# Attention: head images stacked for two batches in one set of DMAs, maxima of three heads in one reduction, TensorE's step reordered

## The reference

```python
    B, T, C = x.shape
    qkv = x @ w_attn
    q, k, v = jnp.split(qkv, 3, axis=-1)
    ...
    q = _apply_rope(q, emb)
    k = _apply_rope(k, emb)
    scale = HEAD_DIM ** (-0.5)
    wei = jnp.einsum('bhqd,bhkd->bhqk', q, k) * scale
    causal = jnp.tril(jnp.ones((T, T), dtype=bool))
    wei = jnp.where(causal[None, None], wei, -jnp.inf)
    wei = jax.nn.softmax(wei, axis=-1)
    out = jnp.einsum('bhqk,bhkd->bhqd', wei, v)
    out = out.transpose(0, 2, 1, 3).reshape(B, T, C)
    out = out @ w_proj
```

## Time and profile before

| what | us |
|---|---|
| median of 3 runs | 334.37 |
| lowest and highest run | 330.97 and 334.4 |
| the profiled execution | 332.37 |
| its span | 330.6 |
| stage A and what is ahead of it | 0 to about 123 |
| stage B | about 123 to 247 |
| feed-forward block | about 247 to the end |

### The profile page before, as it was taken

The page is one execution under the profiler, slowest core; times in us unless marked ns, Lnnn a source line. Parts: engine busy times, 40 slices in busy tenths (PEclk is TensorE's granted clock), DMA queues, the critical chain, the costliest instruction groups (busy, mean ns, idle before and its releaser), DMA issues.

```text
span 330.6 us, 6296 instructions
## 1 busy us (share of the span) xinstructions
PE 253.5 (77%) x1878; PEld 191.1 (58%) x1878; DVE 241.3 (73%) x674; ACT 138.2 (42%) x300; POOL 133.8 (40%) x133
## 2 busy tenths in 40 slices
PE   0129896976868785779998879899876969797881
PEld 0029795976757764546776667767554545454440
DVE  2999589999899988984687656767546674747453
ACT  0320022132232232355665546666765754545350
POOL 1640425758668776563232322333486430000000
PEclk9999999799999998957999979999999887896978
DMA  5900000000008950022433434341000001011011
GB/s 139 234 0 1 26 24 24 2 25 6 20 24 116 115 57 0 0 53 62 106 76 87 97 87 93 84 108 24 2 2 1 2 0 36 0 36 36 2 48 37
DMA packets 25847, 15.61 MB, mean 47 GB/s; under 512 B 3872, under 2 KB 25696, under 8 KB 25824
## 3 DMA queue, kind: packets, MB, share of 16 engines
q1 hardware_dynamic: 23568, 14.04, 21.2%
q10 hardware_dynamic: 2256, 1.29, 1.8%
HBM read 4.26 MB, written 1.57 MB: 18 GB/s over the span
## 4 chain that ended last, share of the span: by engine, by line
DVE 33%; PE 29%; SPq 18%; issue 10%; DMA 3%; ACT 2%; POOL 2%; DVEq 1%; ACTq 0%; POOLq 0%
SPq L364 13%; PE bank L1413 8%; DVE xs_ring L817 7%; PE bank L1428 7%; DVE xl_ring L868 6%; SPq L380 5%; DVE xn_ring L804 3%; DVE rest_ring L843 2%; DVE parts L1066 2%; DMA rad_bc<-in_L_conv_radius 2%; DVE gn_st L748 2%; PE bank L1306 2%; PE bank L1194 2%; PE bank L1264 1%; DMA stack<-nmax_t 1%
## 5 line engine op out<-in xcount | busy, mean ns | idle before, releaser
L921 DVE TENSOR_REDUCE nmax<-bank 128x1 f32<-128x128 f32 x192 | 55.0, 348 | 29.3 <-PE bank L1267 28.9
L490 POOL TENSOR_SCALAR_AFFINE_SELECT pt_ring<-pt_ring 128x512 f32<-128x512 f32 x48 | 30.5, 637 | 62.4 <-ACT pt_ring L618 62.4
L1168 PE MATMUL bank<-xs_ring,toep 128*128 128x192 f32 x256 | 51.3, 347 | 2.2 <-DVE xs_ring L817 2.2
L618 ACT ACTIVATE pt_ring<-bank 128x384 f32<-128x384 f32 x96 | 41.7, 487 | 20.0 <-PE bank L1283 19.3
L1168 PEld LDWEIGHTS bank<-xs_ring,toep 128*128 128x128 f32 x256 | 45.2, 203 | 3.8 <-issue 2.5
L1264 PE MATMUL bank<-stack 96*128 96x128 bf16 x192 | 35.2, 260 | 0.7 <-ACT nmax_t L607 0.4
L1267 PE MATMUL bank<-mask,ident 128*128 128x128 bf16 x192 | 35.2, 231 | 0.0
L1281 PE MATMUL bank<-stack 97*128 97x256 bf16 x96 | 23.7, 290 | 11.0 <-DMA stack<-nmax_t 7.2
L868 DVE TENSOR_SCALAR xl_ring<-tok,ln_mv,ln_rstd 128x96 f32<-128x96 f32 (+1 forms) x32 | 27.6, 920 | 2.1 <-POOL ln_rstd L467 2.1
L1031 DVE TENSOR_REDUCE amax<-parts 128x1 f32<-128x384 f32 x30 | 16.4, 552 | 16.8 <-ACT parts L672 15.7
L1413 PE MATMUL bank<-parts,w_b 96*128 96x384 f32 x60 | 28.6, 626 | 0.0
(11 more groups left out here) (145 smaller groups left out, 503.2 us busy)
## 6 DMA issues: line engine op xcount, KB each, us to landing
stack<-parts SPq DMA_DIRECT2D x96, 96.0 KB, 3.4
x_ring<-in_x SPq DMA_DIRECT2D x8, 192.0 KB, 2.5
out<-xs_ring SPq DMA_DIRECT2D x5, 288.0 KB, 2.6
stack<-in_x SPq DMA_DIRECT2D x2, 384.0 KB, 6.1
stack<-in_x ACTq DMA_DIRECT2D x2, 384.0 KB, 10.8
stack<-nmax_t SPq DMA_DIRECT2D x32, 1.5 KB
cst<-in_const SPq DMA_DIRECT2D x1, 384.0 KB, 11.3
w_in<-in_L_ffn_W ACTq DMA_DIRECT2D x2, 144.0 KB, 12.1
```

The source lines that it names most:

```text
L490: nc.gpsimd.affine_select(out=v, in_=v, compare_op=ALU.is_ge, fill=0.0, base=0, pattern=[[0, 2], [0, 2], [1, P]], channel_multiplier=-1).t ...
L618: nc.scalar.activation(pt_ring[:, s, h, :], bank[:, 3 + h % 2, 0:T + P], ACT.Exp, scale=float(HD) ** -0.5).then_inc(s_exp, 1)
L921: last = nc.vector.tensor_reduce(nmax[:, n0 % 2, HEADS * t + h:HEADS * t + h + 1], bank[:, h % 3, first:first + (t + 1) * P], op=ALU.max, ...
L1168: nc.tensor.matmul(dst, w, xs_ring[:, s, p, k].rearrange("p b c -> p (b c)"), start=(k == 0 and p == 0), stop=False)
```

## The change

It has three parts.

1. **Images of two batches.** `parts` is laid out by pairs of batches, so that the same part of two neighbouring batches lies side by side, and `stack` has three slots of two batches. `stack_images(n)` issues six DMAs of 192 KB for batches n and n+1, for even n. The runs of memory that a DMA reads are twice as long (512 bf16 values, 1 KB, where they were 512 bytes; 2 KB in the one combination whose q and k parts are neighbours). SP's order is now, for n = 4, 6, ..., 14: `max_row(n-3)`, the wait for both batches, `stack_images(n)`, `max_row(n-2)`.
2. **Maxima of three heads.** `maxima` takes heads 0 to 2 or 3 to 5 in two reductions over three banks, and `scores_q` waits once for three heads. The transposed maxima go to bank 5 instead of bank 2 (except those of batch 0), with waits that keep them apart from `transpose_o`'s output there.
3. **A step's order.** TensorE's `step_b` is `scores_k` 0, three heads of `scores_q`, `scores_k` 1, `transpose_max`, `weighted_values`, `transpose_norm`, three heads of `scores_q`, `scores_k` 2, `project_out`, `transpose_o`. DVE normalises batch n-2's output at the start of step n, where it did n-1's in the middle of it. ACT does the second pair of exponentials before it copies `o_ring`.

```diff
-        stack = sb("stack", [P, RING, HEADS, 2, T], BF16)
+        stack = sb("stack", [P, RING // 2, HEADS, 2, 2, T], BF16)
...
-        parts_v = parts[0:C, :].rearrange("c (b s k n) -> c (b s) k n", b=B, s=2, k=3)
+        parts_v = parts[0:C, :].rearrange("c (j s k u n) -> c (j s) k u n", j=PAIRS, s=2, k=3, u=2)
...
-            def stack_image(i, n0):
+            def stack_images(i, n0):
                 b, slot = n0 + RING * i, n0 % RING
                 for r, (kp, qp) in enumerate(SLOTS):
-                    q_part = parts[0:C, ds((b * 6 + qp) * T, T)]
-                    src = bass.AP(q_part.tensor, q_part.offset, [q_part.ap[0], [(3 + kp - qp) * T, 2], [1, T]])
-                    dst = stack[r * HD:(r + 1) * HD, slot, :, :, :].rearrange("d h s n -> d (h s n)")
-                    sp.dma_start(dst, src).then_inc(s_stack[slot], 16)
+                    q_part = parts[0:C, ds((b * 6 + 2 * qp) * T, 2 * T)]
+                    src = bass.AP(q_part.tensor, q_part.offset,
+                                  [q_part.ap[0], [(3 + kp - qp) * 2 * T, 2], [1, 2 * T]])
+                    dst = stack[r * HD:(r + 1) * HD, slot // 2, :, :, :, :].rearrange("d h s b n -> d (h s b n)")
+                    sp.dma_start(dst, src).then_inc(s_stack[slot // 2], 16)
...
-            for n in range(4):
-                stack_ready(0, n)
-                stack_image(0, n)
+            for n in (0, 2):
+                images_ready(0, n)
+                stack_images(0, n)
             max_row(0, 0)
-            def step_b(i, n0):
-                max_row(i, n0 - 3)
-                stack_ready(i, n0)
-                stack_image(i, n0)
-            run(sp, step_b, start=4, first=4, unroll=RING, laps=2, last=B)
+            with sp.Fori(0, 2) as i:
+                for n in (4, 6, 8):
+                    max_row(i, n - 3)
+                    images_ready(i, n)
+                    stack_images(i, n)
+                    max_row(i, n - 2)
...
-            def maxima(i, n0, h):
+            def maxima(i, n0, g):
                 b = n0 + RING * i
-                dve.wait_ge(s_sq, HEADS * b + h + 1)
-                if h == 0:
+                dve.wait_ge(s_sq, HEADS * b + 3 * (g + 1))
+                if g == 0:
                     wait(dve, s_mt, b - 1)
                 for t in range(NT):
-                    first = t * P
-                    last = nc.vector.tensor_reduce(nmax[:, n0 % 2, HEADS * t + h:HEADS * t + h + 1],
-                                                   bank[:, h % 3, first:first + (t + 1) * P],
+                    first, k = t * P, HEADS * t + 3 * g
+                    last = nc.vector.tensor_reduce(nmax[:, n0 % 2, k:k + 3], bank[:, 0:3, first:first + (t + 1) * P],
                                                    op=ALU.max, axis=AX.X, negate=True)
```

191 lines of the change are left out of this document (98 added, 93 removed).

## The result

| | before | after |
|---|---|---|
| median, 4 runs each | 334.38 us | 370.88 us |
| lowest and highest | 330.97 and 334.96 | 367.46 and 372.81 |
| the profiled execution | 332.37 | 367.46 |
| its span | 330.6 | 365.7 |

The ratio is 1.110, with a 95% interval of 1.099 to 1.122: 11% slower. The forecast was 352 us with a range to 362, so the sign was right and the size was half of it. In the profiled executions the spans differ by 35.1 us, where the forecast had 19.8.

A forecast was written before the change was run, and what follows sets the result against it. SP's issues were taken to bound the kernel, with DMA bytes next; +1.0 up to step 2, +20.2 in five rounds and -1.4 behind step 12 made +19.8 on 332.37: 352 us, range 343 to 361.

The forecast's parts named there:

- new waits: 0: Waits of `transpose_max` and `transpose_o` for bank 5 and ACT's cast: 0 us; prologue shift 0, bounds -0.5 and +1.
- maxima of three heads: 0: DVE's reductions gain 0.5 us a step, worth 0; coarser exchange with TensorE costs 0, given 5 us slack a round.
- the -1.4 behind step 12: Behind step 12 no images are in the way, so waits of 0.7 us in two steps go: -1.4 us.
- X: Stage B, time until all six image DMAs have landed: 2.7 us beside the bytes plus 9.4 of bytes, 12.1 us.
- Rival A: Transfers keep pace with their issue; a DVE loop of 5.6 us a step is near: round 11.3, 323 us, chance 0.22.
- B: Engines keep an undisturbed image's rate: bytes take 6.4 us, round 13.2, 332 us, no change; chance 0.12.
- C: SP still bounds, larger DMAs issued at half the pace (1.4 us each): round 12.3 us; no case of its own.
- The round of 17.0: Two batches in stage B: 4.1 us, X of 12.1 and 0.8 for the clock make 17.0, where 12.95 was.
- 4.1 and 0.8 for the clock: Even step's start to image issue: 2.1 us to the odd batch's row, 2.0 on SP; 0.8 for TensorE's lower clock.
- bounds of 0 and 1.7: Range for TensorE's clock loss in a round, whose 1.7 us part would take 3.4; 0.8 was taken.
- bounds of -0.5 and +1 for the prologue: Batch 1's scores behind `transpose_max` and its cast can shift by about 0.25 us either way: put at 0.

The follow-up runs named there:

- images alone: Kernel before with only the images of two batches, its old maxima and old order kept: 354.8 us, ratio 1.071.
- order alone: Kernel before with only the maxima of three heads and the new order of TensorE, DVE and ACT, images and SP's order as before: 343.3 us, ratio 1.033.

## Why the forecast had the sign right and half of the size

The difference of the spans, by the forecast's own terms:

| | forecast | images alone | order alone | the change |
|---|---|---|---|---|
| up to step 2 | +1.0 | +1.9 | +4.1 | +4.6 |
| five rounds | +20.2 | +20.2 | -0.2 | +24.7 |
| from step 12 to the last `project_out` | -1.4 | +1.1 | +5.0 | +6.5 |
| feed-forward block, unchanged | 0 | -1.4 | -0.6 | -0.6 |
| sum | +19.8 | +21.7 | +8.3 | +35.1 |

The five rounds with the images alone are 20.2 of the 35.1 us, as forecast. What failed are the terms put at nothing, *new waits: 0* and *maxima of three heads: 0*, and the -1.4 behind step 12: the stretches in which they stand are 3.6 and 7.9 us longer than forecast. In the rounds 4.5 us are missing, most of them in X.

*What bounded before*: right. Rows off SP's queue, and a step falls from 6.48 to 6.04 us. But TensorE's own step was put at 5.4 us. Its busy time in ten steps, 58.15 us, already said 5.8.

*The bytes pass at 118 GB/s in a burst, whatever their runs*: right. 1.66 us for each DMA of 192 KB, where 1.67 was forecast, and half of the bytes end the long rounds. The Trainium skill (page "DMA: Bandwidth & Descriptors", section "Bandwidth") gives 435 GB/s as the fabric's ceiling for SBUF to SBUF. No burst here comes near it, with large or small DMAs. Rival A fell, the one that this rate would have favoured, and its other leg fell too: a step of the new order takes 6.07 us where nothing holds it up, not 5.6. Rivals B and C fell as well: the last image lands 8.8 us after its issue, and SP issues the large ones at the old pace.

*The round of 17.0*: 17.9 was measured. From the step's start to the issue of the set the forecast had 4.1 and 0.8 for the clock, and the five rounds have 4.04, 5.36, 5.47, 5.48 and 4.81, 5.03 in the mean. The walk through `scores_k` 0, three heads, `scores_k` 1, the transpose, the cast and SP was right: 4.04 is the first round, at full clock. The clock then adds 1.3 to 1.4 in three rounds and 0.8 in the last, inside the forecast's bounds of 0 and 1.7. Behind the 4.57 us wait the granted clock is 0.50 for all of the next 6.4 us, not for half of them, as it was behind the wait of 1.68 us. The mis-sized term is X: 12.86 us from the first issue to the next even step in the round from 200.81, not 12.1. The first image lands after 4.1 instead of 3.7, and step n+2 begins 0.4 behind the last landing, for which the sum had no term. This is 3.8 us in five rounds.

That the images alone give rounds of 16.98, the forecast's number, is luck. There the transpose stands behind two heads and the set follows the step's start after 4.08 us, 0.8 less than the forecast's 4.9 for the new order, and the longer landing fills that up. The forecast walked the new order's path to the odd batch's row, but did not ask what that path costs against the old order's. The run with `transpose_max` put back answers: 0.9 us a round. In the trace the walk to the cast's end takes 3.6 us at half clock (195.33 to 198.89), where the old order needs 2.4 (191.29 to 193.68).

*New waits: 0*, and *maxima of three heads: 0*. These are the steps that failed. The reason given was that DVE has 5 us of slack in each round. That is true in the rounds and says nothing of the steps outside them. In step 0 the exchange of three heads (two reductions, 948 and 555 ns, in these rows)

```profile
L922 DVE TENSOR_REDUCE nmax<-bank 128x3 f32<-128x768 f32 x32 | 30.3, 948 | 0.0
...
L922 DVE TENSOR_REDUCE nmax<-bank 128x3 f32<-128x384 f32 x32 | 17.8, 555 | 64.2 <-PE bank L1262 64.2
```

makes TensorE wait for 1.41 us, and the run with single heads shows 1.1 us of this as its cost. The bounds of -0.5 and +1 for the prologue were taken from one cast of 0.25 us; from stage A's wait to step 0 are 12.55 us, where 10.98 were, so +1.6 (+0.9 in the run with `transpose_max` put back, whose code is the same up to there). Another 1.9 of the 4.6 us up to step 2 are in step 1, where the first large set lands late; the images alone show 1.8. And the tail was not looked at: DVE's new order was read from the loop, and what is called between the loop's last steps (`second_stats`, `largest_hidden`) was not laid beside it. This is 4.2 us, by both runs that put the normalisation first.

*The waits of 0.7 us behind step 12 go: -1.4*. With the images alone 12.72 us pass from step 12 to 14, where 11.65 did. The wait goes, but step 12 itself begins behind an idle time and runs slowly. In the change it is 13.06 us, +1.4 instead of -1.4, and the clock is 0.76 in step 12.

Open are three things: what lengthens the prologue and step 1 of the new order once its maxima are taken head by head (1.8 us up to step 2); what the large DMAs lose in a round against small ones (0.4 us); and by what way the images' bytes delay a row of maxima in another queue. The runs show only that they do.

## What to carry to other kernels

When a queue bounds by its issues, look for another queue first: moving the small DMAs off SP gave 1.5%, where fewer and larger DMAs cost 7%. Transfers that were hidden because they were spread out are no longer hidden in a burst, and a small DMA that someone waits for lands with the burst ahead of it. Where an order is changed in a loop, read the prologue and the code behind the loop on each engine as closely as the loop: here the stretches ahead of step 2 and behind step 12 were over a quarter of the loss. And ask what the bound behind the present one is: a free queue for SP was worth 0.44 us a step at most.

## What the hardware showed that I had not expected

- The row of maxima on ACT's queue was held up about as long as on SP's. With sets of 192 KB DMAs issued around it on SP, TensorE started 6.3 to 8.0 us after its issue had ended, in the five steps that waited for it. On SP's own queue it was 5.5 to 6.7 in the change's five rounds, and with images of 96 KB and the row on ACT's queue 3.3.
- Two DMAs of half a row cost ACT 1.39 to 1.56 us of its own time in the loop and GpSimd 1.03. SP spent 4.3 us on six image DMAs, whether of 96 or 192 KB.
- Twelve DMAs of 96 KB and six of 192 KB passed a burst at much the same rate, 110 to 121 and 122 GB/s, though the runs of the first are half as long.
- The same feed-forward code took 76.2 to 81.5 us, at a granted clock of 0.88 to 0.79.
